# Layer norms inside the stages ahead of them, and weights loaded one stage earlier, in a fused four-block transformer kernel

## The reference, cut to what matters

```python
x = x + attention_a(layernorm(x))      # softmax over a 512x512 channel matrix
x = x + ffn(layernorm(x))              # 8 experts of width 256: 2 shared, 6 routed
x = x + attention_b(layernorm(x))      # gated delta rule, 16 heads of 128, two causal-scan states
x = x + ffn(layernorm(x))              # the same weights again

def layernorm(x, eps=1e-05):
    m = mean(x, -1); v = var(x, -1)
    return (x - m) / sqrt(v + eps)
```

## Time and profile before

| | us |
|---|---|
| median of 3 runs | 3431.48 (3424.70 to 3431.81) |
| the profiled execution | 3426.05 |
| its span, first to last instruction | 3424.3 |
| TensorE (matmul) busy | 3244.6, 95% |
| VectorE busy | 2156.9, 63% |
| ScalarE busy | 1480.1, 43% |
| mean granted TensorE clock | 0.974 |

### The profile page before, as it was taken

How to read it: one execution, slowest core, us unless ns; L and a number is a source line. 1 busy time by engine, 2 the same in 40 slices (tenths; PEclk the granted TensorE clock), 3 DMA queues, 4 the chain that set the end, 5 groups by cost and what they waited for, 6 DMA issues and landing times. The chain is left out here.

```text
span 3424.3 us, 78381 instructions
## 1 busy us (share of the span) xinstructions
PE 3244.6 (95%) x33424; PEld 1534.5 (45%) x33424; DVE 2156.9 (63%) x3546; ACT 1480.1 (43%) x3401; POOL 125.6 (4%) x457
## 2 busy tenths in 40 slices
PE   7989999996889999999999999999999868999999
PEld 4444444443444444444444444444444434444443
DVE  2354524415788888889878988878898625451441
ACT  2031101104456756766675676567667533110110
POOL 0000000000000000000000000000000000000000
PEclk9999999998989999999999999999999878999999
DMA  3022222114101111121121211101211012222121
GB/s 120 0 64 69 74 86 68 55 49 165 34 27 33 57 52 40 39 70 43 31 67 40 63 40 48 42 28 55 67 42 33 18 68 89 74 75 85 62 55 62
DMA packets 99289, 195.72 MB, mean 57 GB/s; under 512 B 10248, under 2 KB 35464, under 8 KB 96384
## 3 DMA queue, kind: packets, MB, share of 16 engines
q1 hardware_dynamic: 98944, 190.71, 17.5%
HBM read 173.64 MB, written 17.04 MB: 56 GB/s over the span
## 5 line engine op out<-in xcount | busy, mean ns | idle before, releaser
L1624 PE MATMUL psum<-dl_xt,dl_wqkv 128*128 128x512 f32 x1536 | 762.6, 620 | 9.7 <-DVE dl_qkv L1268 9.6
L1268 DVE SCALAR_TENSOR_TENSOR dl_qkv<-psum,dl_par,dl_qkv 128x511 f32<-128x511 f32 (+2 forms) x576 | 428.7, 744 | 32.5 <-ACT dl_tails L1107 23.5
L481 PE MATMUL psum<-xnt_sb,wmats 128*128 128x512 f32 x896 | 408.3, 593 | 2.2 <-DVE f_partial L707 2.2
L1624 PEld LDWEIGHTS psum<-dl_xt,dl_wqkv 128*128 128x128 f32 x1536 | 262.6, 190 | 265.0 <-issue 229.0
L481 PE MATMUL psum<-f_token_sums,wmats 128*128 128x512 f32 x672 | 306.8, 592 | 0.0
L707 DVE TENSOR_TENSOR f_partial<-f_partial,psum 128x512 f32<-128x512 f32 x112 | 76.9, 687 | 310.2 <-PE psum L481 308.8
L481 PEld LDWEIGHTS psum<-xnt_sb,wmats 128*128 128x128 f32 x896 | 169.4, 190 | 218.0 <-issue 212.0
L596 ACT ACTIVATE f_partial<-psum 128x512 f32<-128x512 f32 x32 | 19.1, 597 | 550.6 <-PE psum L481 550.6
L1631 PE MATMUL psum<-dl_wo,dl_sg 128*128 128x512 f32 x512 | 256.7, 620 | 0.3 <-DVE dl_sg L1471 0.3
L1103 ACT ACTIVATE dl_qkv<-psum,dl_par 128x512 f32<-128x512 f32 x192 | 148.9, 776 | 194.5 <-PE psum L1624 194.5
L537 PE MATMUL psum<-f_wdown,f_hidden_a 128*128 128x512 f32 x512 | 224.3, 592 | 0.0
(11 more groups left out here) (217 smaller groups left out, 4713.2 us busy)
## 6 DMA issues: line engine op xcount, KB each, us to landing
dl_wqkv<-in_dw_qkv SPq DMA_DIRECT2D x192, 256.0 KB, 2.6
f_wdown<-in_wdowns SPq DMA_DIRECT2D x64, 512.0 KB, 3.5
wmats<-in_wmats SPq DMA_DIRECT2D x56, 512.0 KB, 3.5
dl_wo<-in_dwo SPq DMA_DIRECT2D x16, 1024.0 KB, 5.2
f_weights_b<-f_weights_by_expert SPq DMA_DIRECT2D x24, 512.0 KB, 9.5
x_sb<-in_x SPq DMA_DIRECT2D x4, 1024.0 KB, 9.1
x_after_experts<-x_sb SPq DMA_DIRECT2D x16, 256.0 KB, 2.6
xn_transposed<-xnt_sb SPq DMA_DIRECT2D x4, 1024.0 KB, 5.9
```

Source lines behind the costliest of these rows:

```text
L481: ins = pe.matmul(ps[:, bank, :], wm[:, m % WRING, block, k, :], moving[:, k, :], start=(fresh and k == 0), stop=(last_of and k == 1), ski ...
L1268: tap_ = lambda dl: dve.scalar_tensor_tensor(y_[:, dl:TT], ps[:, bank, 0:TT - dl], par[:, h, 4 * a + 3 - dl:4 * a + 4 - dl], y_[:, dl:TT], ...
L1624: last = pe.matmul(ps[:, bank, :], wq[:, n % RING, m, :], xt[:, u // HG % 2, m, :], start=(m == 0), stop=(m == KC - 1))
```

## The change

Six things are changed:

1. n2 is gone. In attention, tiles are normalized, turned and copied into `xnt_sb` in the loop of the last step; the turn of tile n stands behind the products of tile n+2 on TensorE, and ScalarE takes one square root per tile.
2. n3 is gone. In f1 the statistics of the first 1024 tokens are taken while the second pair runs; tiles 0 to 7 are normalized behind the U matrices of that pair and turned behind `products(18)` to `products(25)`; they are copied straight into the delta stage's `dl_xt`, which now lives before it. Tiles 8 to 11 follow in the last row of down products, tiles 12 to 15 at the end. Tiles 8 to 15 still go through HBM.
3. The attention weights are loaded in n1, the router in attention (for f2: in n4), and dl_wab and the first three projection matrices in f1.
4. `DRING` goes from 4 to 3.
5. The statistics of a 512-token part no longer stand in `put_out`.
6. Logits, probabilities and ranks live in parts of `act_g` and `weights_b` that are free at that time.

The diff, cut:

```diff
-WRING, DRING = 3, 4
+WRING, DRING = 3, 3
...
 def attention_stage(...)
             def _(sp):
-                for n in ("wk", "wq", "wo", "wvt"):
-                    sp.dma_start(w[n][:, :, :], dram[n].rearrange("(k p) n -> p k n", p=P)).then_inc(w_in[n], 16)
                 ahead(sp)
...
-                for i in range(NT):
...
+                for i in range(NT + 2):
+                    if i < NT:
...
+                    if i >= 2:
+                        n = i - 2
+                        pe.wait_ge(xn_ready, n + 1)
+                        if n >= 2:
+                            pe.wait_ge(xn_taken, n - 1)
+                        for k in range(KC):
+                            last = pe.transpose(ps[:, 4 + n % 2, k * P:(k + 1) * P], xn[:, n % 2, k * P:(k + 1) * P],
+                                                cst[:, K_ID:K_ID + P])
+                        last.then_inc(xn_turned, 1)
...
+                for i in range(NT + 1):
+                    if i < NT:
+                        act.wait_ge(var_ready, i + 1)
+                        act.activation(rstd[:, i:i + 1], mv[:, i, 1:2], ACT.Sqrt,
+                                       bias=cst[:, K_EPS5:K_EPS5 + 1]).then_inc(std_ready, 1)
+                    if i >= 1:
+                        n = i - 1
+                        act.wait_ge(xn_turned, n + 1)
+                        act.activation(xnt[:, :, n * P:n * P + P], ps[:, 4 + n % 2, :].rearrange("p (k t) -> p k t", k=KC),
+                                       ACT.Copy).then_inc(xn_taken, 1)
...
+                    if i >= 1:
+                        n = i - 1
+                        one = slice(n, n + 1)
+                        dve.wait_ge(std_ready, n + 1)
+                        o.done(dve.reciprocal(rstd[:, one], rstd[:, one]))
+                        o.wait()
+                        o.done(dve.scalar_tensor_tensor(shift[:, one], mv[:, n, 0:1], -1.0, rstd[:, one], ALU.mult, ALU.mult))
+                        o.wait()
+                        if n >= 2:
+                            dve.wait_ge(xn_turned, n - 1)
+                        dve.tensor_scalar(xn[:, n % 2, :], x_sb[:, n, :], rstd[:, one], shift[:, one],
+                                          ALU.mult, ALU.add).then_inc(xn_ready, 1)
...
 def ffn_stage(...)
+                if ahead is not None:
+                    ahead(sp)
                 group(0, 0)
...
-                sp.wait_ge(stored, 16 * NT)
+                last = 16 * NT
+                if normed_to is not None:
+                    for e in range(2, TN):
+                        sp.wait_ge(xn_taken, 4 * e + 4)
+                        sp.dma_start(normed_to[1][e], xnt[:, :, e * TT:e * TT + TT]).then_inc(stored, 16)
+                        last += 16
+                sp.wait_ge(stored, last)
...
+                            if normed_to is not None and MATS + 4 <= m < MATS + 12:
+                                turn_x(m - MATS - 4)
...
+                        if normed_to is not None and p + 1 == PAIRS and 2 <= g < 6:
+                            turn_x(g + 6)
                     bias(2 * p + 1)
+                if normed_to is not None:
+                    for i in range(12, NT):
+                        turn_x(i)
...
+                def norm_between(m):
+                    if normed_to is not None and m == MATS + 3:
+                        deviation(0, 8)
+                    if normed_to is not None and MATS + 4 <= m < MATS + 12:
+                        take_x(m - MATS - 4)
...
+                        if m == MATS + 1:
+                            statistics(1)
+                        if m == MATS + 3:
+                            factors(1, 0, 8)
+                        if MATS + 3 <= m < MATS + 11 and kind == "U":
+                            normalize(m - MATS - 3)
+                            normalize(m - MATS - 2)
...
 def delta_stage(...)
-                sp.dma_start(xt[:, 0], xnt_dram[0]).then_inc(s["xt_in"], 16)
-                sp.dma_start(wab[:], d["dwa"]).then_inc(s["wab_in"], 16)
-                sp.wait_ge(s["xt_in"], 16)
-                sp.wait_ge(s["wab_in"], 16)
-                for n in range(RING):
-                    load_proj(n)
...
+        def delta_ahead(sp):
+            sp.dma_start(wab[:], d["dwa"]).then_inc(wab_in, 16)
+            for n in range(RING):
+                sp.dma_start(wq[:, n], d["dw_qkv"][0, n]).then_inc(wq_in[n], 16)
...
-            norm_stage(nc, "n2_", x_sb, xnt, ps, cst, meanvar=mv2)
...
-            norm_stage(nc, "n3_", x_sb, xnt, ps, cst, store_to=xnt_dram, meanvar=mv3)
```

More of the change, by code:

```diff
@@ L557, in turn_weights, with turn_x @@
                                  cst[:, K_ID:K_ID + P]).then_inc(wt_ps, 1)
+                def turn_x(i):
+                    pe.wait_ge(xn_ready, i + 1)
+                    if i > 0:
+                        pe.wait_ge(xn_taken, i if i <= 8 else i - 1)
+                    bank = 3 if i < 8 or i % 2 == 0 else BA
+                    for k in range(KC):
+                        last = pe.transpose(ps[:, bank, k * P:(k + 1) * P], xn[:, i % 2, k * P:(k + 1) * P],
+                                            cst[:, K_ID:K_ID + P])
+                    last.then_inc(xn_turned, 1)
                 pe.wait_ge(wr_in, 32)
@@ L616, in _ @@
                     act.activation(out_b[:, 0], out_b[:, 0], ACT.Silu, bias=table[:, c0:c0 + 1]).then_inc(silued, 1)
+                    norm_between(m)
+                if normed_to is not None:
+                    for e in range(2, FN):
+                        deviation(4 * e, 4 * e + 4)
+                        for i in range(4 * e, 4 * e + 4):
+                            take_x(i)
             @block.vector
@@ L730, in put_out, with statistics, factors, normalize @@
                         dve.tensor_tensor(x_sb[:, i, :], ps[:, 4 + i % 4, :], x_sb[:, i, :], ALU.add).then_inc(acc_read, 1)
-                    if meanvar is not None:
-                        for i in range(4 * e, 4 * e + 4):
-                            dve.wait_ge(acc_read, i + 1)
-                            step(dve.bn_stats(st[:, i, :], x_sb[:, i, :]))
-                            dve.bn_aggr(meanvar[:, i, :], st[:, i, :])
+                def statistics(e):
+                    for i in range(4 * e, 4 * e + 4):
+                        dve.wait_ge(acc_read, i + 1)
+                        step(dve.bn_stats(st[:, i, :], x_sb[:, i, :]))
+                        dve.bn_aggr(mv[:, i, :], st[:, i, :]).then_inc(var_ready, 1)
+                def factors(n, first, end):
+                    dve.wait_ge(std_ready, n)
+                    step(dve.reciprocal(rstd[:, first:end], rstd[:, first:end]))
+                    step(dve.scalar_tensor_tensor(shift[:, first:end], mv[:, first:end, 0], -1.0, rstd[:, first:end],
+                                                  ALU.mult, ALU.mult))
+                def normalize(i):
+                    if i >= 2:
+                        dve.wait_ge(xn_turned, i - 1)
+                    dve.tensor_scalar(xn[:, i % 2, :], x_sb[:, i, :], rstd[:, i:i + 1], shift[:, i:i + 1],
+                                      ALU.mult, ALU.add).then_inc(xn_ready, 1)
                 for n in range(2):
@@ L956, in delta_stage @@
         read = {b: sem(f"dl_read{b}") for b in range(4, 8)}
-        w_in = [sem(f"dl_w_in{n}") for n in range(RING)]
         def wait_full(eng, *job):
@@ L1801, in program @@
             xnt = c2.enter_context(nc.sbuf_tensor("xnt3_sb", [P, KC, T], F32))
-            wm, wm_in, ahead = expert_weights(c2, 2)
+            loaded, ahead = expert_weights(c2, 2)
             norm_stage(nc, "n4_", x_sb, xnt, ps, cst, source=x3, ahead=ahead)
-            ffn_stage(nc, "f2_", x_sb, xnt, ps, cst, d, out, wm, wm_in)
+            ffn_stage(nc, "f2_", x_sb, xnt, ps, cst, d, out, loaded)
 def arrange(inputs):
```

143 lines of the change are left out of this document (93 added, 50 removed).

## The result

| | before | changed kernel |
|---|---|---|
| median | 3429.99 us | 3395.9 us |
| lowest to highest, four runs each | 3424.70 to 3431.81 | 3389.33 to 3399.28 |
| ratio | | 0.9901, interval 0.9882 to 0.9920 |
| profiled execution, span | 3426.05, 3424.3 | 3396.07, 3394.3 |

The gain is 34.1 us at the medians and 30.0 in the two profiled executions. The forecast was 3398 us with a range of 3390 to 3410 and a sum of 30.6.

What follows compares the result with a forecast made beforehand. TensorE is busy 95%, so only its idle or low-clock time can be won. Terms 7.0 + 8.4 - 4.2 + 17.3 + 2.1 = 30.6 us give 3395.4 (profiled) and 3400.9 (median); forecast 3398, range 3390 to 3410.

Steps and rivals of the forecast that it cites:

- Start of attention: Attention's first products: early weights start TensorE 4.85 us sooner and first eight records save 2.2; gain 7.0, lower end 4.8.
- rival A: TensorE's clock falls in the shorter pauses too, costing 2.2 and 1.1 us; gain 27.3, 3401 us; chance 0.10.
- Last step and n2: Attention's last step to the logits: turns add 6.2, tail 5.2, barrier 0.8; 12.2 us instead of 20.6, gain 8.4.
- rival B: Attention's loop becomes a chain of waits, 1 us per tile, 16 in all; gain 14.6, 3414 us; chance 0.05.
- Inside f1: Within f1: twelve added turns cost 5.3 us, the 1.09 wait of matrix 15 goes; net -4.2.
- Ring: Down matrices in f1 and f2: with three slots a load has 13.8 us and needs 3.5; cost 0.
- End of f1 to delta: From VectorE's start on f1's last result to delta's first product: 18.2 us instead of 35.5; gain 17.3.
- The upper end: Border from f1 to delta: last 1 MB store has less traffic ahead, 1.5 us better; gain 18.8.
- Start of f2: Logits of f2: TensorE starts at 2845.25 instead of 2847.38 us; gain 2.1, lower end 1.
- 1.9 faster were the clock high throughout: Logits of f1: left at 5.32 us for 32 records, but possibly about 1.9 us faster at a high clock.
- a longer delta stage: Sign against the forecast: the untouched delta stage, 2000 us, has itself become longer.

## Why the prediction was right

It was right step by step, with sizes off in the last step of attention, at the end of f1 and at f2. That the sum of the profiled pair came out within 0.6 us is luck: misses of opposite sign cancel.

- **Start of attention**, predicted 7.0, measured 7.38 in the profiled pair (0.33 of it n1, which ended that much earlier) and 7.2 alone. The choice between 2.2 us and nothing for the clock was right for most executions. The trace supports both sides, though: in two of eight the pause of 2.48 us lowered the clock. The row of 1.66 us that I took as the nearer one says what can happen, not what always does. Such an execution pays 5.07 instead of 3.60 us on its first eight records, 1.5 and not the 2.2 of rival A. The Trainium skill (TensorE: Matmul & The Clock Gate, Part 1) says that the low clock is the default and activity releases it. Read as strictly as in rival A, that fits two of these eight executions and not the other six.
- **Last step and n2**, predicted 8.4, measured 9.32. The turn at 0.44 and the period of 3.9 are as forecast and no turn waits inside the loop, so rival B did not occur. The thirteen turns took 177.47 - 116.56 - 55.20 = 5.7, as forecast. What was too large is the tail behind the last product: a turn, 5.2 and the barrier's 0.8 make 6.4, and it took 5.57. The turn of 0.4 was one term too many: it stands directly behind the last product (177.30), while VectorE already works on the last tile. VectorE's chain and the copies took 4.7 instead of 5.2, to the last copy's end at 182.16.
- **Inside f1**, predicted -4.2, measured -3.95. The wait of 1.09 went, so the twelve turns cost 5.0 instead of 5.3; no wait came in its place. Of the waits left in f1 the two of L577, 0.85 us each, are those for `put_out`, as forecast. A third, of L521 for a sum (0.57 us, early in the first pair), is not, but it was there before, with the same 0.57.
- **Ring**, predicted 0, measured 0.
- **End of f1 to delta**, predicted 17.3, measured 18.46. From VectorE's start to the end of the fourth copy it took 769.18 + 0.60 - 758.25 = 11.5, as predicted. The step that was off is the last one: from the last copy's end to the stage, 6.7 carried over from before, 775.25 - 769.78 = 5.5 measured. The upper end had this, with the reason that less traffic stands ahead of the store. The rows agree: the last 1 MB store took 5.74 us to land before (793.28 to 799.02), where an earlier one landed at 796.56, and takes 4.41 now, where the one before it has landed at 765.78.
- **Start of f2**, predicted 2.1, measured 5.03. The start itself gained 2.2. The rest, 2.8, is the clock: the 32 records of the logits took 3.62 instead of 6.45. The prediction gave this possibility to f1 ("1.9 faster were the clock high throughout") and left it out here. It is no fixed gain either: the two later executions of the changed kernel had 5.24 there, while the four variants without transposes in n4 all had 3.55. Before the change the four executions had 5.92 to 6.38.
- **Delta**, no term. Its 6.2 us were scatter that the single profile before hid. The prediction named a longer delta stage as something that would show it wrong. That sign was badly chosen, since one execution of that stage cannot carry it. The range, which was made from the terms and from 7 us of spread among runs, covered it.

The two last points are 2.9 too little gain and 6.2 too much, and with +0.4, +0.9, +0.25 and +1.2 on the other terms the sum moves from 30.6 to 30.0. Without delta the stretches of the profiled pair gained 36.2, more than the prediction's upper end of 34.5, because the logits of f2 ran at the upper clock there; at the medians the gain was 34.1, and in the later comparison 3428.47 - 3396.84 = 31.6.

Open: what in a pause of 2.48 us decides whether the clock falls, and what starts a delta stage with more low-clock time. Neither was varied alone. The turns inside f1 and the router's early load for f2 were not tried by themselves either; their terms are read from the rows of before and after.

## What to carry to other kernels

Cost a border between stages by walking from the last result to the next stage's first product and adding what is left on that chain. Five of six terms came out within 1.2 us that way; a small load issued with the stage cost 3.7 us, a last store of 1 MB instead of 256 KB 1.8. Behind each removed wait look at the clock as well: it was worth 2.1 us on attention's first eight records and 2.8 on the logits of f2, with n2 fused the logits of f1 took 1.7 longer than in the one execution with n2 restored, and a few unused transposes held it, at no cost where they ended before the next work was ready. Before a few microseconds of a long, untouched stage are given to a change, compare that stage in several executions of the kernel before; here it moved by 8.5 us on its own.

## What the hardware showed beyond that

- One pause, the same instructions up to there, two outcomes: behind 2.48 us of idle PE the first eight records took 3.60 us in six executions and 5.0 in two. The two had a window with a granted clock of 0.50.
- Thirty-two records of the logits take 3.55 us, start to start, at the upper clock (2.4 GHz) and 5.02 to 6.38 with the lower one in part. Fifty-six transposes of 128x128 take 6.30 us, 0.11 each, and hold the clock up: the product behind them took 3.67 instead of 6.26.
- The delta stage's length varies by 8.5 us at the same instructions (1987.0 to 1995.5) and by 12 over all twelve executions, with 95 to 125 us of it at the lower clock; I had taken it as fixed.
- A table load of ScalarE takes 1.28 us (L1166 above), and nobody waits for it: it stands beside delta's first product.
